# Tail tiles turned three ahead over four PSUM banks, with three output banks and default rows ahead of a tile's copies

## The reference

```
x = x + relu(gnn(layernorm(x), adj))
x = x + ffn(layernorm(x))

gnn:  Xw = X @ Wv + bv;  e = leaky_relu(sj + si + ab)      # sj, si: Xw @ aw, per column and row
      T = A * exp(e) / (rowsum + 1e-12)
      H = X @ Wk0 + T X @ Wk1 + T T X @ Wk2 + biases
ffn:  logits = xf @ switch_w.T + switch_b                  # 16 experts
      route = argmax, p = max softmax
      pos = place of the token in its expert's queue; keep = pos < 1228
      y = expert_w[route] @ xf + expert_b[route]
      out = where(keep, y, xf) * p
```

## Time and profile before

| what | value |
|---|---|
| median of three runs | 755.63 us |
| the profiled execution's own time | 753.94 us |
| its span, first to last instruction | 752.2 us |
| TensorE, VectorE, ScalarE, GpSimd busy | 713.5, 641.0, 479.5, 444.8 us |
| mean granted TensorE clock | 0.988 of full speed |
| DMA | 100.12 MB, 133 GB/s on average |

### The profile page before, as it was taken

One profiled execution on the slowest core, in us unless ns is written; L12 is line 12 of the kernel. 1 busy time (PEld: TensorE's weight loads), 2 busy tenths in 40 slices (PEclk: granted clock), 3 DMA queues, 4 the chain that ended last, 5 costly groups with the idle time before them and its releaser, 6 DMA issues.

```text
span 752.2 us, 18567 instructions
## 1 busy us (share of the span) xinstructions
PE 713.5 (95%) x4857; PEld 632.3 (84%) x4857; DVE 641.0 (85%) x3101; ACT 479.5 (64%) x1508; POOL 444.8 (59%) x526
## 2 busy tenths in 40 slices
PE   8999999999999999999999999999999999958873
PEld 7788887889999998999898999999999989847762
DVE  6899999998988998999889899889998888776553
ACT  3567776766676666666666666666676676544541
POOL 4435554456666666766656666676666665665563
PEclk9999999999999999999999999999999999999998
DMA  9623544444444334445434433444443323244430
GB/s 279 174 77 105 161 147 134 142 134 135 135 154 136 116 129 154 155 143 156 140 129 148 146 115 116 147 150 144 144 144 115 123 81 100 95 150 142 124 102 0
DMA packets 93001, 100.12 MB, mean 133 GB/s; under 512 B 10395, under 2 KB 85208, under 8 KB 92898
## 3 DMA queue, kind: packets, MB, share of 16 engines
q1 hardware_dynamic: 77012, 65.96, 29.5%
q0 software_dynamic: 13008, 30.07, 10.9%
q10 hardware_dynamic: 2880, 2.92, 1.4%
HBM read 49.92 MB, written 54.72 MB: 139 GB/s over the span
## 4 chain that ended last, share of the span: by engine, by line
PE 86%; DVE 8%; issue 2%; POOL 1%; another core or an unknown queue 1%; ACT 0%; POOLq 0%; DVEq 0%
PE ps_z12a L1320 11%; PE ps_z12b L1320 11%; PE ps_lgb L1320 9%; PE ps_z0a L1320 8%; PE ps_z0b L1320 7%; PE ps_lga L1435 5%; PE ps_z0a L1403 4%; PE ps_z0b L1403 4%; PE ps_z12b L1382 4%; PE ps_xt L1422 3%; PE ps_xt L1350 3%; PE ps_z12a L1382 3%; PE ps_lgb L1464 3%; PE ps_t L1396 2%; PE ps_t L1371 2%
## 5 line engine op out<-in xcount | busy, mean ns | idle before, releaser
L555 POOL DMA_INDIRECT out<-lent,tok x143 | 145.5, 1018 | 158.4 <-DVE lent L1236 136.1
L542 POOL DMA_INDIRECT rowbuf<-rows,idx x128 | 129.7, 1013 | 54.4 <-issue 30.3
L620 ACT CAST xth<-ps_xt 128x256 fp32r<-128x256 f32 x128 | 47.7, 373 | 112.9 <-PE ps_xt L1350 110.7
L497 POOL TENSOR_SCALAR x<-xin,nm,r 128x256 f32<-128x256 f32 x128 | 84.5, 661 | 24.7 <-PE ps_xt L1350 18.8
L695 ACT ACTIVATE x<-rin 128x256 f32<-128x256 f32 x143 | 86.9, 608 | 3.1 <-issue 1.6
L1435 PEld LDWEIGHTS ps_lga<-swc,xft 128*128 128x128 f32 x512 | 76.4, 190 | 10.7
L677 ACT ACTIVATE od<-rows,oc,oa 128x256 f32<-128x256 f32 x128 | 77.1, 602 | 0.1
L835 DVE TENSOR_TENSOR xtl<-ps_xt,xth 128x256 fp32r<-128x256 f32 x128 | 53.9, 421 | 16.5 <-ACT xft L669 16.3
L493 POOL TENSOR_TENSOR r<-ve,mhalf 128x4 f32<-128x4 f32 x31 | 32.2, 1039 | 56.9 <-ACT ve L655 56.4
L1435 PE MATMUL ps_lga<-swc,xft 128*128 128x16 f32 x512 | 65.6, 241 | 0.0
L641 ACT ACTIVATE e<-ps_t,svs 128x128 f32<-128x128 f32 x128 | 47.0, 367 | 17.6 <-PE ps_t L1396 15.1
(11 more groups left out here) (215 smaller groups left out, 2393.0 us busy)
## 6 DMA issues: line engine op xcount, KB each, us to landing
rin<-rowbuf SPq DMA_DIRECT2D x143, 130.0 KB
out<-od SPq DMA_DIRECT2D x32, 512.0 KB
xin<-in_x SPq DMA_DIRECT2D x31, 512.0 KB, 4.1
ain<-in_adj SPq DMA_DIRECT2D x32, 256.0 KB, 4.5
ewr<-in_ewT SPq DMA_DIRECT2D x16, 256.0 KB, 2.6
out<-lent,tok POOLq DMA_INDIRECT x143
rowbuf<-rin ACTq DMA_DIRECT2D x1, 2080.0 KB, 13.5
rowbuf<-rows,idx POOLq DMA_INDIRECT x128
```

Of the source, the lines that this page charges most:

```text
L497: pool.tensor_scalar(x0[:, g % 2, :], xin[:, g % BODY, :], nm1[:, q, g % G:g % G + 1], r1[:, q, g % G:g % G + 1], ALU.add, ALU.mult).then_ ...
L542: pool.indirect_dma_start(out=rowbuf, out_offset=bass.IndirectOffsetOnAxis(ap=idx[:, i:i + 1], axis=0), in_=rows[:, r, :], in_offset=None, ...
L555: pool.indirect_dma_start(out=out.rearrange("g n d -> (g n) d"), out_offset=bass.IndirectOffsetOnAxis(ap=tok[:, i % RY:i % RY + 1], axis=0 ...
```

## The change

- TensorE's `tile(i)` in the tail turns tile i+3 instead of i+2. Turned rows lie in four banks by i % 4: `ps_xt`, `ps_z12b`, `ps_tile`, `ps_z12a`. A turn waits for the low half of tile i-4.
- Outputs lie in three banks: `ps_z0b`, `ps_z0a`, `ps_log`, by (i - 97) % 3. `expert(i)` waits for the finish of tile i-3.
- Turn 100 waits once for the last copy out of `ps_xt` (`s_xfe`), expert 99 once for the last reading of `ps_log` (`s_lgr`).
- ScalarE's `tile(i)` is high i+2, norm i+4; VectorE's is low i+2, finish i.
- The default rows of ScalarE stand ahead of a tile's high and norm, from tile 99 to tile 103; one more stands between high 100 and norm 102.

```diff
-        ps_bx = [*ps_z12, ps_tile]
-        ps_by = ps_z0
+        ps_bx = [ps_xt, ps_z12[1], ps_tile, ps_z12[0]]
+        ps_by = [ps_z0[1], ps_z0[0], ps_log]
...
+        def rows_bank(i):
+            return ps_tile if i < WOVEN else ps_bx[i % 4]
+        def out_of(i):
+            return ps_tile[:, D:2 * D] if i < WOVEN else ps_by[(i - WOVEN) % 3][:, 0:D]
...
# scalar engine
             def tile(i):
-                if i + 1 < NT:
-                    high(i + 1)
-                if i + 3 < NT:
-                    norm(i + 3)
+                if i + 2 < NT:
+                    high(i + 2)
+                if i + 4 < NT:
+                    norm(i + 4)
...
             norm(WOVEN + 4)
+            high(WOVEN + 3)
+            default_rows(IT, G30 + 2)
+            norm(WOVEN + 5)
             for i in range(WOVEN + 2, NT):
-                tile(i)
-                g = G30 + 2 + i - WOVEN - 2
+                g = G30 + 3 + i - WOVEN - 2
                 if g < BODY:
                     default_rows(IT, g)
+                tile(i)
...
# vector engine
             def tile(i):
-                if i + 1 < NT:
-                    low(i + 1)
+                if i + 2 < NT:
+                    low(i + 2)
                 finish(i)
...
             last_step(NG - 1)
+            low(WOVEN + 3)
             for i in range(WOVEN + 2, NT):
...
# tensor engine, turn(i)
-                    pe.wait_ge(b_lo, i - 2)
+                    pe.wait_ge(b_lo, i - 3)
                 if i == WOVEN:
                     pe.wait_ge(s_z1, B)
-                if WOVEN <= i < WOVEN + 3 and i % 3 == 2:
+                if i == WOVEN + 1:
                     pe.wait_ge(b_fin, WOVEN)
+                if i == WOVEN + 3:
+                    pe.wait_ge(s_xfe, B)
...
# tensor engine, expert(i)
-                if i >= WOVEN + 2:
-                    pe.wait_ge(b_fin, i - 1)
+                if i == WOVEN + 2:
+                    pe.wait_ge(s_lgr, NG)
+                if i >= WOVEN + 3:
+                    pe.wait_ge(b_fin, i - 2)
...
# tensor engine, tile(i), behind expert(i)
-                if i + 2 < NT:
+                if i <= WOVEN + 1:
                     turn(i + 2)
+                if i > WOVEN and i + 3 < NT:
+                    turn(i + 3)
```

More of the change, by code:

```diff
@@ L699, in high @@
                 act.wait_ge(b_xt, i + 1)
-                src = ps_tile if i < WOVEN else ps_bx[i % 3]
-                act.copy(xth[:, xr(i), :], src[:, 0:D]).then_inc(b_hi, 1)
+                act.copy(xth[:, xr(i), :], rows_bank(i)[:, 0:D]).then_inc(b_hi, 1)
             def tile(i):
-                if i + 1 < NT:
-                    high(i + 1)
-                if i + 3 < NT:
-                    norm(i + 3)
+                if i + 2 < NT:
+                    high(i + 2)
+                if i + 4 < NT:
+                    norm(i + 4)
             def first_moments(lo, signal):
@@ L1220, in low @@
                 dve.wait_ge(b_hi, i + 1)
-                src = ps_tile if i < WOVEN else ps_bx[i % 3]
-                dve.tensor_tensor(xtl[:, xr(i), :], src[:, 0:D], xth[:, xr(i), :].bitcast(F32),
+                dve.tensor_tensor(xtl[:, xr(i), :], rows_bank(i)[:, 0:D], xth[:, xr(i), :].bitcast(F32),
                                   ALU.subtract).then_inc(b_lo, 1)
@@ L1227, in finish @@
                 c, r = i % RY, i % RI
-                src = ps_tile[:, D:2 * D] if i < WOVEN else ps_by[i % 2][:, 0:D]
+                src = out_of(i)
                 dve.wait_ge(b_y, i + 1)
@@ L1455, in turn @@
                 else:
-                    pe.wait_ge(b_lo, i - 2)
+                    pe.wait_ge(b_lo, i - 3)
                 if i == WOVEN:
                     pe.wait_ge(s_z1, B)
-                if WOVEN <= i < WOVEN + 3 and i % 3 == 2:
+                if i == WOVEN + 1:
                     pe.wait_ge(b_fin, WOVEN)
+                if i == WOVEN + 3:
+                    pe.wait_ge(s_xfe, B)
                 pe.wait_ge(b_xf, i + 1)
-                dst = ps_tile if i < WOVEN else ps_bx[i % 3]
+                dst = rows_bank(i)
                 for t in range(KT):
@@ L1488, in expert @@
                 pe.wait_ge(b_lo, i + 1)
-                y = ps_tile[:, D:2 * D] if i < WOVEN else ps_by[i % 2][:, 0:D]
+                y = out_of(i)
                 c = xr(i)
```

## The result

On one chip, ten runs of each: 753.35 us (751.63 to 754.16) against 755.5 us before (754.14 to 757.51), a ratio of 0.9974, interval 0.9965 to 0.9982. The change gains some 2 us where 13.3 were forecast, and the time lies above the range of 736.7 to 751.

A forecast was written before the change was run, and what follows sets the result against it. The prediction took a round trip with late TensorE completions to bound the tail. A gain of 18.0 us at GpSimd's pace, less 1.7 at the tail's start and 3.0 for late completions, gave 13.3: 742.3 us, range 736.7 to 751.

The forecast's parts named there:

- What bounds the kernel: Tail, tiles 110 to 142: a round trip, no engine's work, sets 1.61 us a tile; TensorE's completions seen 1.7 late.
- late completions from tile 110 on: Tiles 110 to 142: late completions stay, costing some 0.25 us about 11 times, 3.0 us in all, between 0 and 10.5.
- The start of the tail: Scatters 98 to 110: turns wait for row loads, and scatter 110 comes at 685.9; 1.7 us given back, 0 to 7.4.
- The floor: Tail scatters at GpSimd's 1.285 us a tile: the last begins at 725.3 instead of 743.24, a gain of 18.0 us.
- the walk through the queues: Start of the tail: following the engines' queues put scatter 110 at 685.9, where GpSimd's pace alone gave 684.2.
- Banks: Tail PSUM: four banks for turned rows and three for outputs add waits for earlier tiles, none coming last; no cost.
- the new one-time waits: Tail start: waits for the last ps_xt copy and logits scaling, over by 657.46, before turn 100 at 661.91; cost nothing.
- the row loads (B): Rival: SyncE's row loads set the tail's pace at 1.43 us a tile; 747.8 us, chance 0.08.
- D: Rival: short stops in every tile keep TensorE's clock low from tile 110; 9.8 us slower, 765.4 us, chance 0.04.
- A: Rival: tail completions are late by the tile, not the microsecond; about 1.5 us a tile, 750.1 us, chance 0.11.
- C: Rival: nothing gained; the stop moves within the same round trip, a tile still takes 1.61 us; 755.6 us, chance 0.05.

The follow-up runs named there:

- before_again: The kernel before, unaltered, run once more on another chip for its profile beside a changed kernel with a one-column memset behind late scatters: 758.31 us.

## Why the prediction was wrong

**What bounds the kernel** was half right: a round trip between TensorE and the engines behind it, with late completions in it. The sentence that failed is "Why they are late no row tells; I take it as a property of this tail". The trace did tell: the scatters of 686.54 to 689.12 stand in a row, and the release in the earlier trace rows follows its end by 0.7 us. A completion is not late by 1.7 us. On chips of the first kind one that comes behind the second scatter of a row waits, in the regular rows, until the row has ended. The row is as long as the tiles that VectorE can finish on one release: the three (before: two) whose products were waiting, and one more whose products end during the second scatter.

**The term "late completions from tile 110 on"** is the one that was wrong in size: 3.0 us, measured 51.14 - 41.1 = 10.0, at its upper bound of 10.5. The lead of one more tile made a row of four scatters out of one of three, so a regular row costs 4 x 1.285 + 1.4 = 6.54 us where it cost 3 x 1.285 + 1.2 = 5.06: 1.64 a tile instead of 1.69. (Both traces have a few irregular rows, which bring the means to 1.60 and 1.61.) A lead stretches the row, and each row pays for one stop. On chips of the second kind the term is nothing: 684.10 to 725.20 is 32 x 1.285. The working of the 3.0 has a slip besides: 1.7 less 1.17 and 0.12 is 0.41 and not 0.25, and 11 times that is 4.5. The 1.17 us a tile of TensorE was too long as well, 1.06 from 704.17 to 706.28; neither changes the verdict.

**The start of the tail** was forecast to give back 1.7 us, between 0 and 7.4. On the first kind of chip the 12 tiles from 98 to 110 took 22.29 us where the floor has 15.4: 6.9. On the second kind, where completions are not held up, it took 17.95 (666.15 to 684.10): 2.5, so the walk through the queues was near for what it counted. Of the other 4.4 us one stop of the same kind is in the trace (the scatters of tiles 107 and 108 start at 685.36 and 688.56, 1.9 us over GpSimd's pace), which I had let begin at tile 110 alone; the rest no run separates from the lower clock there (below). The sum is then 18.0 - 6.9 - 10.0 = 1.1, and the last scatter is 1.0 earlier.

**The floor**, a last scatter at 725.3, was right as a floor and wrong as a thing that the lead could reach on these chips. On the second kind of chip the last one starts at 725.20; that this is the forecast's own number is luck, for tile 98 starts 2.6 us earlier there and the tail takes 2.5 longer than the floor. By its time of 734.6 the kernel before gets there as well, though its own trace was not taken there: with a completion seen at once, a lead of one tile is enough, and the change is worth nothing or slightly less (1.0014 of before, 1.0004 to 1.0023).

**Banks, the new one-time waits, the row loads (B)**: nothing of the first two shows among the waits of the tail, and row loads cost 3.0 us in 682:741, in two waits. **D**, the clock, did not come in the steady part:

```profile
682.00:741.00 59.00, 46.88 (x322) 40.46 (x322) 32.62 (x107) 29.55 (x70) 35.03 (x37) 0.97 0.34 98
```

```profile
682.00:741.00 59.00, 43.66 (x318) 39.84 (x318) 31.03 (x110) 27.34 (x66) 35.78 (x38) 0.97 0.34 97
```

The first line is of the kernel before, the second of the changed one: a granted clock of 0.97 in both (0.91 and 0.99 in 700:720, 1.00 and 0.92 in 682:700). At the start of the tail it was lower in the changed kernel, 0.76 against 0.88 in 656:670 and 0.72 against 0.86 in 670:682, but in before_again the kernel before itself shows 0.50 in 670:682, so these traces do not tell whether the change did it. What the Trainium skill tells in the section that stood beside D ("TensorE: Matmul & The Clock Gate", "A second HAM failure mode: psum-queue depth-cycling"), of a kernel that lost its clock over and over as it cycled through PSUM banks, is not what held this one up: the steady part has the same clock with one more output bank in the cycle. Rivals **A** (750.1) and **C** (755.6) lie on both sides of the result, 753.35. A had the nearest reading, late by the tile; C had the words, "the stop moves to another place of the same round trip". Together they had a chance of 0.16, too little: I had seen both engines released within 0.05 us of each other, "as by one blocked path", and did not ask what blocked it.

## What to carry to other kernels

When several engines are released in the same moment, look at every engine, and not only at those in the chain, for what ended just before. GpSimd was the last one served in this loop, none of TensorE's waits in 682:741 names it, and its scatters were what held the loop up. Lead and buffers help against a delay of fixed length; against one that lasts as long as the backlog they buy a longer backlog. What took most of the stops away here was fewer scatters (0.9772 of before with 15 of the last 31 left out, so with rows missing from the output) or wider gaps between them, and the gap of 0.82 us cost more than it won (1.0054); a form that gains and keeps the output was not found. A tuned kernel's few tenths of a per cent are worth measuring on more than one chip: this change is 0.9974 on one and 1.0014 on another.

## What the runs showed of the hardware

- A scatter of 128 rows takes GpSimd 0.98 us and the next starts 0.30 us later, 1.285 us from one to the next, and as much when every row number is out of bounds and 0.01 MB is moved.
- On chips where the kernel before takes 755 to 757 us, in rows of scatters with 0.30 us between them, TensorE's completions up to the second scatter are seen by VectorE and ScalarE at once when they are free (703.21 seen at 703.24). Those behind it are not seen until some 0.7 to 0.9 us after the last of the row in the regular rows (704.46 seen at 707.31), with a few exceptions. With 0.39 us between the scatters the stops stay; it needs no data to be moved (0.01 MB, the same stops); with a gap of 0.82 us they are gone.
- On other chips, with the same program and the same 0.98 us per scatter, nothing of this is seen (704.52 seen at 704.55 in a row of over thirty), and the same kernel takes 734.5 us: 2.8% less.
- From the start of the last scatter to the end of the span 7.8 to 9.0 us pass (729.44 to 737.2, 742.27 to 751.2, 725.20 to 734.2).
- Which part of the chip is shared, whether it is GpSimd's work, the queue's packets or their completions that block it, and why the chips differ, no run here tells.
